# Table set and weight transfers in the expert sublayers of a twelve-sublayer decoder kernel

## The reference

```python
def _sinkhorn(log_alpha, iters=3):
    for _ in range(iters):
        log_alpha = log_alpha - logsumexp(log_alpha, axis=-1, keepdims=True)
        log_alpha = log_alpha - logsumexp(log_alpha, axis=-2, keepdims=True)
    gates = jnp.exp(log_alpha)
    return gates / (jnp.sum(gates, axis=-1, keepdims=True) + 1e-08)

scores = (jnp.einsum('btd,ed->bte', x, router_w) + router_b) / temp
gates = _sinkhorn(scores)
topk_vals, topk_idx = jax.lax.top_k(gates, K)
topk_gates = topk_vals / (jnp.sum(topk_vals, axis=-1, keepdims=True) + 1e-08)
g = relu(jnp.einsum('btd,edf->btef', x, wg)); p = jnp.einsum('btd,edf->btef', x, wp)
all_out = jnp.einsum('btef,efd->bted', g * p, wo)
gathered = jnp.take_along_axis(all_out, topk_idx[..., None], axis=2)
return x + jnp.sum(gathered * topk_gates[..., None], axis=2)
```

## Time and profile before

| | us |
|---|---|
| median of 3 runs | 1985.57 |
| lowest and highest run | 1977.89, 1986.81 |
| the profiled execution, its own time | 1987.53 |
| its span, first to last instruction | 1985.7 |
| PE busy | 1468.4 (74%) |
| DVE busy | 1222.3 (62%) |
| ACT busy | 934.6 (47%) |
| POOL busy | 380.2 (19%) |
| mean granted clock of TensorE | 0.850 |

### The profile page before, as it was taken

One profiled execution on the slowest core, in us unless ns is written; L12 is line 12 of the kernel. 1 busy time (PEld: TensorE's weight loads), 2 busy tenths in 40 slices (PEclk: granted clock), 3 DMA queues, 4 the chain that ended last, 5 costly groups with the idle time before them and its releaser, 6 DMA issues. The chain is left out here.

```text
span 1985.7 us, 32127 instructions
## 1 busy us (share of the span) xinstructions
PE 1468.4 (74%) x11270; PEld 894.7 (45%) x11270; DVE 1222.3 (62%) x4051; ACT 934.6 (47%) x2009; POOL 380.2 (19%) x404
## 2 busy tenths in 40 slices
PE   5997978844763669996446599999974993677874
PEld 2554434433551443443224356666654882443432
DVE  7776378844233647776666477777664223557876
ACT  4554266642221235554632177777752440126655
POOL 3320021013645005320011000000002546002100
PEclk9999999965995779999557599999995995669995
DMA  3320023112451003320010000000003662003300
GB/s 117 57 44 2 0 34 48 23 32 64 140 120 36 1 26 64 52 44 19 0 55 1 11 6 7 6 7 12 1 8 91 203 182 56 1 16 44 54 2 21
DMA packets 58686, 84.52 MB, mean 43 GB/s; under 512 B 8352, under 2 KB 46496, under 8 KB 58016
## 3 DMA queue, kind: packets, MB, share of 16 engines
q1 hardware_dynamic: 48384, 46.54, 11.5%
q0 software_dynamic: 10144, 35.93, 6.4%
HBM read 51.18 MB, written 9.18 MB: 30 GB/s over the span
## 5 line engine op out<-in xcount | busy, mean ns | idle before, releaser
L638 DVE TENSOR_REDUCE maxs<-ps 128x4 f32<-128x1024 f32 x192 | 234.8, 1223 | 62.5 <-PE ps L966 60.9
L794 ACT ACTIVATE L_xattn_probs<-ps 128x1024 f32<-128x1024 f32 x192 | 196.5, 1024 | 85.1 <-PE ps L991 80.8
L3386 ACT ACTIVATE wide_pr<-wide_sc,wide_nm 128x256 f32<-128x256 f32 x256 | 126.9, 497 | 12.7 <-DVE wide_nm L3321 12.2
L966 PE MATMUL ps<-keys,L_xattn_qs 64*128 64x256 bf16 x768 | 75.3, 274 | 38.4 <-DVE maxs L638 31.9
L1007 PE MATMUL ps<-L_xattn_probs,values 128*32 128x256 f32 x1536 | 102.8, 385 | 0.0
L3293 DVE CUSTOM_DVE_ANT_0 wide_sc<-ps,wide_mask 128x256 f32<-128x256 f32 x256 | 93.8, 420 | 9.6 <-PE ps L3411 8.6
L3316 DVE COPY wide_prT<-ps 128x512 f32<-128x512 f32 x64 | 44.3, 692 | 83.0 <-PE ps L3424 82.8
L1484 POOL DMA_INDIRECT moe_xs<-normed,moe_table x92 | 86.8, 944 | 28.0 <-issue 28.0
L991 PE MATMUL ps<-L_xattn_qm,keys 64*128 64x256 bf16 x768 | 74.6, 271 | 7.3 <-ACT L_xattn_probs L794 7.0
L1890 DVE SCALAR_TENSOR_TENSOR moe_z_sb<-ps,moe_wt,moe_a_sb 128x256 f32<-128x256 f32 x46 | 22.3, 484 | 89.8 <-ACT moe_a_sb L1922 77.1
L3331 DVE TENSOR_SCALAR wide_pr<-wide_pr,wide_inv 128x256 f32<-128x256 f32 x256 | 75.5, 349 | 1.8
(11 more groups left out here) (641 smaller groups left out, 3798.5 us busy)
## 6 DMA issues: line engine op xcount, KB each, us to landing
keys<-L_xattn_k_parts SPq DMA_DIRECT2D x108, 64.0 KB
L_xattn_qs<-L_xattn_q_parts SPq DMA_DIRECT2D x108, 64.0 KB
expert_out<-moe_y SPq DMA_DIRECT2D x46, 128.0 KB
weights<-in_packed_L_xattn SPq DMA_DIRECT2D x2, 1316.0 KB, 7.5
keys<-L_attn_k_parts SPq DMA_DIRECT2D x36, 64.0 KB
L_attn_qs<-L_attn_q_parts SPq DMA_DIRECT2D x36, 64.0 KB
normed<-moe_xn SPq DMA_DIRECT2D x2, 1024.0 KB, 4.8
wide_mask<-in_mask SPq DMA_DIRECT2D x8, 256.0 KB, 2.8
```

Of the source, the lines that this page charges most:

```text
L638: v.tensor_reduce(nm, ps[:, BANK_M:BANK_M + 2, :].rearrange("p j (t n) -> p j t n", t=2), AX.X, ALU.max, negate=True).then_inc(S("m_used"), 1)
L794: a.activation(probs[:, s % RING, :, :, :].rearrange("p j t n -> p j (t n)"), ps[:, BANK_P:BANK_P + 2, :], ACT.Exp, scale=HD ** -0.5)\
L966: mm = pe.matmul(ps[:, BANK_M + j, c + c0:c + c1], qs[half[j], m % 2, gp, q0:q0 + P], kk[half[j], m % 2, gp, b * SEQ + c0:b * SEQ + c1], s ...
L3386: ins = a.activation(pr[:, s % 3, j, qt, :], sc[:, s % 2, j, qt, :], ACT.Exp, bias=nm[:, s % 2, n:n + 1], accum_out=sums[:, s % 2, n:n + 1])
```

## The change

Two things in one diff.

ACT loads the table set `natural_log_exp_and_others`, which holds exponential and logarithm, at the start of its stream in `sinkhorn_moe`.

In both expert sublayers the weights of a slice are no longer fetched by POOL with an indirect DMA over 128 row numbers, but by SP with a plain DMA of 128 rows in a row: SP reads the first number of the slice's column of `rows_of` into a register (`value_load`) and uses it as the start. SP does this for the first four slices when `rows_ready` is signalled, and for slice j + 4 after the store of y of slice j. `fetch` on POOL then holds only the gathers of the tokens' rows; it waits for `normed_stored` and `table_ready` at its start.

```diff
     def fetch(self, g):
 
         C, S = self.C, self.C.sem
-
-        def weights(j):
-            if j >= BUFS:
-                g.wait_ge(S("y_ready"), j - BUFS + 1)
-            g.indirect_dma_start(self.wt[:, j % BUFS, :], None, self.experts,
-                                 bass.IndirectOffsetOnAxis(self.rows_of[:, j:j + 1], 0))\
-             .then_inc(C.routed[f"w_loaded_{j % BUFS}"], 16)
-
-        def rows(j):
+        g.wait_ge(S("normed_stored"), 16)
+        g.wait_ge(S("table_ready"), 1)
+        for j in range(SLICES):
             if j >= BUFS:
                 g.wait_ge(S("x_turned"), j - BUFS + 1)
             for h in range(HALVES):
@@ -1485,24 +1479,24 @@
-        g.wait_ge(S("rows_ready"), 1)
-        weights(0)
-        g.wait_ge(S("normed_stored"), 16)
-        g.wait_ge(S("table_ready"), 1)
-        rows(0)
-        weights(1)
-        rows(1)
-        for j in range(2, SLICES):
-            weights(j)
-            rows(j)
+    def weights(self, sp, j):
+
+        row = sp.value_load(self.rows_of[0:1, j:j + 1], min_val=0, max_val=7 * P)
+        sp.dma_start(self.wt[:, j % BUFS, :], self.experts[bass.ds(row, P), :])\
+          .then_inc(self.C.routed[f"w_loaded_{j % BUFS}"], 16)
 
     def keep(self, sp):
 
         C, S = self.C, self.C.sem
+        sp.wait_ge(S("rows_ready"), 1)
+        for j in range(BUFS):
+            self.weights(sp, j)
         for j in range(SLICES):
             sp.wait_ge(S("y_ready"), j + 1)
             sp.dma_start(C.expert_out[j * SLICE:(j + 1) * SLICE, :].rearrange("(h p) d -> p h d", p=P),
                          self.y[:, j % 2, :].rearrange("p (h d) -> p h d", d=D)).then_inc(C.routed[f"y_stored_{j % 2}"], 16)
+            if j + BUFS < SLICES:
+                self.weights(sp, j + BUFS)
@@ -1748,6 +1742,7 @@
             @block.scalar
             def _(a):
+                a.preload_act_table_set("natural_log_exp_and_others")
                 centre_odd(a, C, xn, shift)
                 copy_turned(a, C, hT)
                 for r in range(ROUNDS):
```

## The result

| | before | after |
|---|---|---|
| median of 6 runs (us) | 1984.76 | 1965.44 |
| lowest and highest | 1977.89, 1986.81 | 1958.89, 1968.64 |
| ratio, with its 95% interval | | 0.9907 [0.9882, 0.9932] |
| the profiled execution, its own time | 1987.53 | 1961.33 |
| its span | 1985.7 | 1959.5 |

The change makes the kernel faster by 19.3 us between the medians, 13.5 to 23.4 by the interval. In a later session the ratio was 0.9888 [0.9866, 0.9910]. The forecast was 1959.5 us in a range of 1953 to 1977: faster, inside the range, and some 6 us too low.

A forecast was written before the change was run, and what follows sets the result against it. It took PE to bound the second expert loop, and POOL's issues plus late slices the first, where nothing was full. 6.8 + 2.3 + 16 + 3.0 = 28.1 us off 1987.5 gave 1959.4, stated as 1959.5, range 1953 to 1977.

The forecast's parts named there:

- The balancing: First router's balancing: table loads exposed on the chain go, 3 x (0.95 + 1.27) + 0.18 = 6.8 us; the added load is hidden.
- rival (3): Balancing: the program still loads a table at each change of function, despite the load ahead; 21.3 us gained, 1966; chance 0.06.
- The first loop: First expert sublayer, 23 slices: shorter POOL issue time and most late slices gone, 16 us gained, bounds 0 and 17.7.
- rival (1): First loop: late slices stay, because traffic or PE itself makes them, not POOL; 14.4 us gained, 1973; chance 0.18.
- (2): First loop: half of the late slices stay; 20.1 us gained in all, 1967; chance 0.19.
- long unbroken runs: First loop: POOL issuing without rest makes slices late; with 2.5 us of issues a slice it would rest 1.1 us in each.
- The start of the first loop: First expert sublayer: two weight issues leave POOL's queue ahead of PE's second pair of transposes, 2.3 us gained.
- The start of the second: Second expert sublayer: 2.3 us from earlier gathers plus 0.7 from rows passing weights on another queue, 3.0 us gained.
- +0.7: Start of the second loop: net of rows passing weights and SP's burst of four transfers, between -2.3 and +1.6 us.
- The second loop: Second expert sublayer: PE bounds it at 4.76 us a slice, so 0 us gained if SP keeps up.
- 1.0 us of margin: First loop, SP's path: weights land 6.9 us after y and are wanted after 7.9 us, so covered by 1.0 us.
- Rival (4): SP's path becomes the bound and the kernel slower; at weights landing 12 us after y, 2006 us; chance 0.07.

The follow-up runs named there:

- the first sublayer alone: The kernel after, but POOL fetches the second expert sublayer's weights as before: 1960.20 us, ratio 0.9856; again, beside after: 1965.25 us, 0.9901.
- the paced gathers: The kernel after, with POOL's 32 gathers after each expert sublayer waiting, from the ninth on, until the pair before has landed: 1937.67 us, ratio 0.9764.
- the spread transfers: The kernel after, where SyncE's second weight transfer waits until the first has landed and the fourth until the second has: 1965.20 us, ratio 0.9909.
- the runs of four: The kernel after, but POOL gathers the rows of two slices together in one run of four issues: 1965.89 us, ratio 0.9913.
- the run with seven loads: The kernel after, with seven register loads by SyncE in place of one per slice from the fifth on: 1998.04 us, ratio 1.0071.

## Why the prediction was right, and where it was off

**The balancing, 6.8 us:** 6.9, as read from the rows, and the load ahead hidden by idle time. The price of 2.66 us a switch that the Trainium skill states ("ScalarE: Activation LUTs", section "What ACT_TABLE_LOAD costs") would have given some 15 by the prediction's estimate; the rows' 1.28 us decided it rightly. With one load left, rival (3) has fallen.

**The first loop, 16 us:** 18.1 in the profiled execution. Over the seven traces of kernels with two issues a slice and one register load (after twice, the first sublayer alone twice, the paced gathers, the spread transfers, the runs of four) it took 78.5 to 81.2 us, against 96.7 before and 96.9 with the table load alone: 15.5 to 18.3 us. That it hangs on POOL's issues, and not on the weights' bytes, is shown by the two runs that keep three issues a slice and take the weights out of POOL's queue or out of the traffic. Rivals (1) and (2) have fallen. The prediction's "long unbroken runs" was right as a direction; it did not say how long a run has to be. The rule behind rival (1) in the Trainium skill ("DMA: Bandwidth & Descriptors", section "Issuing engines are not separate DMA queues"), that another issuer saves no more than time at issue, holds for the transfers, as the starts show, and leaves out what the issues themselves do to other engines: those were 22 x 0.17 = 3.7 us of issue time against 18.1 gained.

**The start of the first loop, 2.3 us:** a loss of 1.1. This step failed, in three terms. The gathers were issued 1.6 us earlier and not 2.3: the table is there 0.34 us after the experts' rows (472.27 and 472.61), not 0.1 as the prediction read it, and POOL starts 0.87 us after the table's end instead of 0.29 after the rows'. Their landing became 1.7 us longer under SyncE's four transfers; this overlap was weighed as a risk for the second sublayer and left out for the first. And from the second transposes to y it took 8.70 us instead of 7.68, nearly all of it a late signal at DVE: PE's own work from the transposes to the end of `down` is 7.67 us against 7.63. The start still has a run of twelve issues, the very thing that the next step of the prediction blamed for late signals, and PE now reaches its first y nearer to that run's end. With rests and the transfers spread that stretch is 6.2 us and the start gains 1.7 us on before (16.9 to 15.2).

**The start of the second, 3.0 us:** a loss of 2.5 in the profiled execution, about 2 over all traces, by the burst: the second transposes come 6.78 us after the issue of their gather instead of 3.27, 3.5 us more where the lower bound allowed 2.3. I took +0.7, the wrong side, and the bound itself was too narrow.

**The second loop, 0 us:** 104.79 and 104.78 us. PE is its bound.

**SyncE:** 0.87 us for the register load and the address, against an upper bound of 0.94; each further load 0.58 us, which agrees with the floor of some 600 ns in the Trainium skill ("DMA: Bandwidth & Descriptors", section "Latency and other measured facts"). The whole path was to have 1.0 us of margin; PE waited for weights three times in the first loop, 3.5 us in all, and never in the second. Rival (4) did not come, and the run with seven loads shows that its bound is the time that SyncE works, which the prediction had not set beside the slice.

**The sum:** 6.9 - 1.1 + 18.1 - 2.5 = 21.4 us by the rows, 19.3 between the medians, against 28.1 forecast from the profiled execution (26 from the median of that time). The two starts miss by 8.9 us (5.3 forecast, 3.6 lost), and the first loop gives 2.1 us of it back. That the profiled execution agrees with the forecast to 2 us is luck: it is 4.7 us faster in stretches that nothing touched.

## What to carry to other kernels

When work leaves a queue, ask what the queue does with the freed time: here it prefetched as far as its buffers let it, in one long run whose end held up the first y. Look for long runs of GpSimd's indirect issues beside waits that the profile calls remote: breaking the run by a wait of 2 us gave 28 us in this kernel, more than the change under study. Such signals can also be late where the profile names PE as the releaser, so compare the wait's end with the recorded end of the matmul. Put such a wait only where the data is far ahead of its use, and price it by its time under traffic.

## What the runs showed of the hardware

Around the end of a long unbroken run of POOL's indirect issues, signals of PE come late at ACT, DVE and POOL, although PE's matmuls are recorded as ended. In runs of two, of three after a rest over 1 us, and of four (2.5 to 5.0 us) two late copies of `xT` were found (0.9 and 1.1 us). Behind runs of six and nine the copies were up to 2.2 us late (1.87 in the earlier trace rows), in a run of eighteen 9.2 us, in one of 32 6.4 us. The releases come 1.3 to 1.7 us after the last issue of a six, 2.0 to 2.2 after a twelve (first y), 3.1 after the eighteen, 2.3 to 5.2 after a 32. One came within the run of 32 (593.12), and signals up to 14 us into the run of eighteen were on time, so the end of a run isn't the only release and its start not the beginning of the trouble. The weights' bytes don't matter (67 and 133 GB/s alike), and no fetch of instructions is seen beside the two waits that were looked at for it. What in the chip holds the signal these runs do not show; nor was a run of five tried. A POOL issue took 0.94 us (the first of a loop up to 1.18) and 0.30 to the next whatever it moved, 64 or 384 KB.

The same eight matmuls took 1.99 us at a granted clock of 1.00 and 3.78 at 0.50, which moved the start of the second loop by 2 us between kernels that do the same there.
